# Four cross-attention layers on one core: the weighing of a batch in one piece, and one Q tile in another slot

## The reference, cut to what matters

```python
# L0 (the first) and L3 (the last), B=16, Sq=100, Sk=361, E=256, H=16, HD=16
Q = (layer_norm(x, g, b) @ wq + bq).reshape(B, Sq, H, HD)
K = (layer_norm(ctx, g, b) @ wk + bk).reshape(B, Sk, H, HD)
V = (layer_norm(ctx, g, b) @ wv + bv).reshape(B, Sk, H, HD)
scores = einsum('bqhd,bkhd->bhqk', Q, K) / sqrt(HD)
attn = softmax(scores, axis=-1)
out = einsum('bhqk,bkhd->bqhd', attn, V).reshape(B, Sq, E)
x = x + out @ wo + bo
```

## Time and profile before

| what | value |
|---|---|
| median of 3 runs | 2113.66 us (2110.45 to 2115.55) |
| profiled execution, its own time | 2111.77 us |
| its span | 2109.8 us |
| TensorE busy (matmul) | 1983.6 us, 94% |
| VectorE, ScalarE, GpSimd busy | 1414.2 (67%), 1276.3 (60%), 562.3 us (27%) |
| L0, scores of the first to the last slot | 36.57 to 339.63 us |
| L3, scores of the first to the last slot | 1807.48 to 2093.08 us |

### The profile page before, as it was taken

The page is one execution under the profiler, slowest core; times in us unless marked ns, Lnnn a source line. Parts: engine busy times, 40 slices in busy tenths (PEclk is TensorE's granted clock), DMA queues, the critical chain, the costliest instruction groups (busy, mean ns, idle before and its releaser), DMA issues. The chain is left out here.

```text
span 2109.8 us, 50608 instructions
## 1 busy us (share of the span) xinstructions
PE 1983.6 (94%) x18664; PEld 1642.0 (78%) x18664; DVE 1414.2 (67%) x2898; ACT 1276.3 (60%) x3249; POOL 562.3 (27%) x676
## 2 busy tenths in 40 slices
PE   7999996978999999999999999999999998899997
PEld 6777775977888888888777787877878876777786
DVE  4777875544545545555577887888788874677775
ACT  3777775545555555555556665666566653677775
POOL 3323320000000000000035755766666651000000
PEclk8999998999999999999999999999999998899999
DMA  5434442021000000000001000000000001344442
GB/s 165 154 125 139 145 131 101 7 73 38 16 8 9 15 9 8 15 9 8 16 1 51 10 15 11 9 10 17 9 10 10 9 1 34 108 131 131 124 124 70
DMA packets 72858, 109.63 MB, mean 52 GB/s; under 512 B 7052, under 2 KB 62508, under 8 KB 72620
## 3 DMA queue, kind: packets, MB, share of 16 engines
q1 hardware_dynamic: 72332, 105.88, 16.5%
q10 hardware_dynamic: 288, 0.51, 0.1%
HBM read 69.18 MB, written 37.19 MB: 50 GB/s over the span
## 5 line engine op out<-in xcount | busy, mean ns | idle before, releaser
L1516 ACT ACTIVATE wide_P<-PS,MX 100x361 f32<-100x361 f32 x512 | 288.3, 563 | 407.3 <-DVE MX L1634 407.3
L1634 DVE TENSOR_REDUCE MX<-PS 100x2 f32<-100x722 f32 x256 | 231.7, 905 | 148.0 <-PE PS L1386 146.5
L615 ACT ACTIVATE L_P<-PS,MX 100x361 f32<-100x361 f32 x512 | 252.7, 565 | 122.0 <-DVE MX L745 122.0
L745 DVE TENSOR_REDUCE MX<-PS 100x2 f32<-100x722 f32 x256 | 219.6, 899 | 45.2 <-PE PS L501 44.9
L1815 POOL TENSOR_TENSOR wide_AC<-wide_T,wide_COSM 128x362 f32<-128x362 f32 x128 | 130.1, 1016 | 336.3 <-ACT wide_T L1465 334.1
L513 PE MATMUL PP<-CON,L_P 100*128 100x100 f32 x1536 | 184.1, 257 | 26.4 <-DVE L_PT L752 17.5
L513 PEld LDWEIGHTS PP<-CON,L_P 100*128 100x128 f32 x1536 | 151.2, 144 | 48.4 <-ACT L_P L615 33.7
L1395 PE MATMUL PP<-CON,wide_P 100*128 100x100 f32 x1536 | 176.5, 251 | 0.0
L1395 PEld LDWEIGHTS PP<-CON,wide_P 100*128 100x128 f32 x1536 | 161.1, 142 | 9.0 <-issue 2.3
L1409 PE MATMUL PS<-wide_PT,wide_V 128*64 128x100 f32 (+1 forms) x3072 | 161.9, 254 | 0.0
L1409 PEld LDWEIGHTS PS<-wide_PT,wide_V 128*64 128x64 f32 (+1 forms) x3072 | 136.8, 137 | 31.0 <-issue 23.3
(11 more groups left out here) (242 smaller groups left out, 5355.2 us busy)
## 6 DMA issues: line engine op xcount, KB each, us to landing
strips<-L_KS SPq DMA_DIRECT2D x256, 90.5 KB
L_KA<-strips SPq DMA_DIRECT2D x64, 362.0 KB, 3.1
C<-ctx_t SPq DMA_DIRECT2D x32, 361.0 KB, 3.1
kept<-L_CTH SPq DMA_DIRECT2D x16, 361.0 KB, 4.7
kept<-L_CTL SPq DMA_DIRECT2D x16, 361.0 KB, 5.5
L_CTH<-kept SPq DMA_DIRECT2D x16, 361.0 KB, 4.2
L_CTL<-kept SPq DMA_DIRECT2D x16, 361.0 KB, 5.0
C<-in_ctx SPq DMA_DIRECT2D x8, 256.0 KB, 3.4
```

The lines of the kernel that those rows point to most:

```text
L615: nc.scalar.activation(P[:, (4 * g + j) % 8, 0:SK], PSB[0:SQ, j, 0:SK], ACT.Exp, bias=MX[:, s % 2, 4 * q + j:4 * q + j + 1], scale=1.0).th ...
L745: nc.vector.tensor_reduce(MX[:, s % 2, 4 * q + 2 * i:4 * q + 2 * i + 2], PSB[0:SQ, 2 * i:2 * i + 2, 0:SK], AX.X, ALU.max, negate=True).the ...
L1516: nc.scalar.activation(P[:, (2 * g + i) % 4, 0:SK], PS_[i][0:SQ, 0:SK], ACT.Exp, bias=MX[:, s % 2, h:h + 1], scale=1.0, accum_out=DEN[:, s ...
L1634: nc.vector.tensor_reduce(MX[:, s % 2, 2 * p:2 * p + 2], PSB[0:SQ, 0:2, 0:SK], AX.X, ALU.max, negate=True).then_inc(Z["maxed"], 1)
```

## The change

The two halves of the weighing become one job `P` in `a_` of the second slot, directly behind the scores and ahead of `turn(g - 1, 1)`. It has 48 matmuls where there were 24 on either side of the transposes. Its waits ask for the copies of the whole batch at once. One Q tile of each batch from 1 on (tile 3 of an even batch from the second on, tile 1 of the next pair in an odd batch) leaves `b_` of the first slot for `b_` of the second. On ScalarE the eviction of `P` stays behind the four exponentials, now by a condition of its own. The order of the jobs decides the PJ banks and what `begin` waits for: `P` now waits for the reading of `O` of the same batch instead of the K tile, and the moved Q tile waits for the K tile instead of `O`.

```diff
@@ jobs_at @@
                     if s + 1 < B:
                         b_.append(("K", s + 1, 1))
+                elif q == 1 and s <= B:
+                    if s == 0:
+                        a_.append(("B", 0, 0))
+                    else:
+                        a_.append(("P", s - 1, 0))
                     if even and 2 <= s < B:
                         b_.append(("Q", s, 3))
                     if not even and s + 1 < B:
                         b_.append(("Q", s + 1, 1))
-                elif q == 1 and s <= B:
-                    if s == 0:
-                        a_.append(("B", 0, 0))
-                    else:
-                        a_.append(("P1", s - 1, 0))
-                        b_.append(("P", s - 1, 0))
                     if first and even and s + 2 < B:
                         b_.append(("X", s + 2, 0))
@@ tensor @@
-                    def weigh(key, half):
+                    def weigh(key):
...
-                        pe.wait_ge(Z["unloaded_even"], NSLOT * s + 2 * half + 2)
-                        pe.wait_ge(Z["unloaded_odd"], NSLOT * s + 2 * half + 2)
-                        dst = begin(key) if half == 0 else bank(key)
-                        for q in (2 * half, 2 * half + 1):
+                        pe.wait_ge(Z["unloaded_even"], NSLOT * s + 4)
+                        pe.wait_ge(Z["unloaded_odd"], NSLOT * s + 4)
+                        dst = begin(key)
+                        for q in range(NSLOT):
...
-                        if half:
-                            last.then_inc(Z["made"], 1)
+                        last.then_inc(Z["made"], 1)
@@ scalar, the loop over the slots @@
-                            if key[0] != "M":
+                            if key[0] not in "MP":
                                 job(key)
...
-                        for key in b_:
-                            job(key)
+                        for key in a_ + b_:
+                            if key[0] == "P" or key in b_:
+                                job(key)
```

More of the change, by code:

```diff
@@ L252, in narrow_layer @@
             PARTS = (0, 2, 1)
-            order = FIRST + [k for sl in SLOTS for part in jobs_at(*sl) for k in part if k[0] != "P1"]
+            order = FIRST + [k for sl in SLOTS for part in jobs_at(*sl) for k in part]
             job_no = {k: n for n, k in enumerate(order)}
@@ L487, in job @@
                     def job(key):
-                        {"W": biases, "C": context_turn, "K": keys, "V": values, "X": query_turn, "Q": queries, "P1": lambda k: weigh(("P",) + k[1:], 0), "P": lambda k: weigh(k, 1), "N": normal_turn,
+                        {"W": biases, "C": context_turn, "K": keys, "V": values, "X": query_turn, "Q": queries, "P": weigh, "N": normal_turn,
                          "M": output_turn, "O": project, "B": output_bias}[key[0]](key)
```

## The result

| | before | changed |
|---|---|---|
| median | 2114.11 us (4 runs, 2110.45 to 2115.55) | 2134.76 us (4 runs, 2131.51 to 2136.07) |
| ratio | 1 | 1.0098, 95% interval 1.0081 to 1.0116 |
| profiled execution, span | 2109.8 us | 2129.4 us |
| TensorE busy | 1983.6 us (94%) | 1975.6 us (93%) |

The change costs 1.0%, 20.6 us by the medians and 19.6 us by the spans. TensorE is busy 8 us less and the kernel is 20 us longer: no work was added, waits were.

What follows compares the result with a forecast made beforehand. TensorE leads, relaying slots with VectorE's copy out of PP. L0 adds 11.9 us and L3 6.2 (11.5 - 5.3), 18.1 in all: profiled 2111.8 becomes 2129.9, plus 1.9 for the median, said as 2132 us; range 2119 to 2142.

Steps and rivals of the forecast that it cites:

- The Q tile leaves the first slot for nothing: First slots: TensorE is freed 0.73 us, but the turn waits for VectorE's copy; gain 1.1 us at most, taken as 0.
- The weighing of 2.17 us: Second slots: first half 1.17 us plus 48 passes at 21 ns, 1.0 us; bounds 2.0 and 2.34 us.
- Second slots held by the copy, 5.03 us, and 5.07 with X: Second slots, L0 and L3: turn-copy-turn chain 5.03 us against TensorE's list of 4.67; with X that list binds, 5.07.
- The rival in which TensorE's list binds: Second slots: 4.67 instead of 5.03 us in 24 slots, 8.6 us less, about 2121 us in all; chance 0.12.
- The third slot of odd batches in L0, 0.43 us: Q tile's low part and two statistics delay the maxima; 0.43 us on each slot held by VectorE, six times.
- the 2.6 of the sum: L0, third slots of odd batches 1 to 11: 0.43 us six times, 2.6 us in all.
- The transfers absorbed, 5.3 us: L3, fourth slots: longer batches let contexts from DRAM arrive in time, so all 5.3 us of TensorE's waits go.
- 11.9 forecast: L0 in all: second slots with X 2.6, without X 6.7, third slots 2.6 us.
- 11.5 in the sum: L3, second slots of batches 1 to 15: 0.77 us longer each; less 5.3 of absorbed waits, 6.2 us for L3.
- waits for transfers that stay: L3: SP's chain through DRAM slows along with the batches, nothing is absorbed, 5.3 us more, 2137 us; chance 0.2.
- the whole tile given back: First slots: without waiting for the copy, 28 shrink by 0.73 us each, 20.4 us, about 2111.5 us; chance 0.06.
- the compensation: Later slots have room that the first two lack, and the time comes out within the measurement; chance 0.05.

Runs made afterwards that it cites:

- the copy was moved: Changed kernel with VectorE's copy of the transposes ahead of the addition of O in first slots; ratio 1.0048 to the kernel before.
- one piece only: Kernel before with the weighing in one piece, the Q tile staying in the first slot; ratio 1.0101, median 2140.3 us beside 2116.8.
- the turn ahead: Changed kernel with the second slot ordered scores, Q tile, turn, weighing in one piece, X; ratio 1.006 to the kernel before.
- the tile only: Kernel before with the Q tile moved to the second slot, the weighing staying in two halves; ratio 1.0041, median 2127.0 us beside 2116.8.
- the early fetch: Kernel before with L3's fetch of a later context issued some 7 us earlier in SP's list, ahead of the strips' landing; ratio 0.9976.
- both edits: Kernel before with context moments and x normalizing behind the first slot's copy, and L3's context fetch earlier in SP's list; ratio 0.9945, median 2105.2 us.
- the changed kernel with the early fetch: Changed kernel with L3's context fetch issued earlier in SP's list; ratio 1.01 to the kernel before, median 2137.8 us.

## Why the prediction was right

The forecast was 2132 us with a profiled execution of 2129.9; measured were 2134.8 and 2131.5.

- *The Q tile leaves the first slot for nothing.* Right: 5.19 and 4.54 us, and 4.86 and 4.21 once the copy was moved. The step that made the prediction was to add 0.15 us to the copy's end and find the turn standing there already.
- *The weighing of 2.17 us.* Measured 2.21 (264.55 to 266.76). The floor of 25 ns that the Trainium skill states ("TensorE: Matmul & The Clock Gate", section "Wait — 56ns, not 53.3ns?") does not hold for this run of passes: 96 of them last 2.28 us, (2.28 - 0.25)/95 = 21 ns apart.
- *Second slots held by the copy, 5.03 us, and 5.07 with X.* Measured 5.06 and 5.10. The rival in which TensorE's list binds fell with one piece only (without its Q tile that list has 0.7 us less and the slot is no shorter) and with the turn ahead (4.75 us).
- *The third slot of odd batches in L0, 0.43 us.* This term of the sum was wrong: measured 0.01. The maxima do start later, 0.90 us after the scores and not 0.63. But I took VectorE's own list to hold that slot to its end, and its copy waits for TensorE's turn. Before, then changed, L0 batch 11:

```profile
264.84 0.68 PE L513 MATMUL PP<-CON,L_P 100*128 100x100 f32 x6
264.99 0.42 DVE L704 TENSOR_TENSOR L_ON<-PJ,RDEN 100x256 f32<-100x256 f32 x1
265.56 0.81 PE L394 MATMUL PJ<-CON,L_CN 128*128 128x128 f32 x6
```

```profile
271.51 0.68 PE L511 MATMUL PP<-CON,L_P 100*128 100x100 f32 x6
271.90 0.42 DVE L703 TENSOR_TENSOR L_ON<-PJ,RDEN 100x256 f32<-100x256 f32 x1
272.24 0.77 DVE L751 COPY L_PT<-PP 128x600 f32<-128x600 f32 x1
272.48 0.81 PE L393 MATMUL PJ<-CON,L_CN 128*128 128x128 f32 x6 [0.29 <-DVE L_ON L703]
```

  The turn ends at 265.52 and 272.19, and the copy starts 0.04 and 0.05 us later; before, the division had been done at 265.41. So the 0.27 us of delay go into slack. But the job `C` behind the turn waits for the division, 0.29 us, and by it the maxima of the fourth slot start 1.37 us after their scores, not 1.25: the fourth slot is 5.05 us against 4.93 (in batch 9 it is the third that has the 0.1 us). That makes some 0.6 us in all for the 2.6 of the sum. In the kernel with the tile only, the maxima are 0.75 us late and 0.49 us of it are paid: the mechanism is there, its slack is about 0.25 us.
- *The transfers absorbed, 5.3 us.* Right, shown by the early fetch, which gains in one kernel and not in the other.
- *Missed: the tails.* The wait for all copies at once costs 1.15 us where nothing else is left to do, and the lower clock adds 2.2 us in this profile. L0's tail has the same wait of 1.1 us.
- *The total is in part luck.* Its parts agree less well than the sum does. L0 came out at 10.2 us for 11.9 forecast. L3 came out at 10.2 for 6.2: 2.6 are the clock in batch 0, and of the other 7.7 the second slots have 12.6 (11.5 in the sum, and two stops of TensorE, 0.65 us, are in them), the fourth slots -5.8 (-5.3 in the sum), first and third slots 0.9. The tail adds 3.3 that the sum did not have, and the start and the middle, nothing in the forecast, are 4.1 shorter. These errors leave 1.5 us between 18.1 and 19.6. What the forecast got right by its mechanism are the distances in the steady slots.

The rivals: waits for transfers that stay fell (none in the profile), the whole tile given back fell (first slots unchanged), and so did the compensation.

## What to carry to other kernels

Where two engines hand a buffer back and forth, find the job that writes it and the job that empties it, and add the signal's way to the end of the latter; if the next start stands there, work taken from the other engine gives nothing. A long job put ahead of the hand-over delays everything that the other engine has to do behind it, while the same job behind the hand-over hides the copy. A wait that a longer kernel no longer shows was not removed, it will be back as soon as the kernel is made faster: mend both together, as the version with both edits does.

## What the runs showed of the hardware

- From the end of VectorE's copy to the start of the waiting TensorE transposes are 0.14 to 0.16 us in the steady slots of every kernel here. A copy that waits for six transposes starts 0.04 us behind their end, which is 0.72 to 0.78 us behind their start at a clock of 1.00 and 1.24 us at 0.50.
- The same work at the two clocks: six transposes last 0.68 to 0.73 us at 1.00 and 1.2 us at 0.50, the weighing in one piece 2.28 us at 1.00 and 4.23 us in the tail of the kernel with one piece only, at a mean of 0.51.
- TensorE sometimes stops, nearly always within a weighing, although it waits for nothing that is shown. It does so a few times in a run, by 0.15 to 2.2 us, at places that change between profiles; the first row is of the changed kernel. The second is the longest, in the changed kernel with the early fetch: its slot takes 8.15 us for 5.06, and the next 6.82 for 4.71 while the granted clock averages 0.61 (1847.5 to 1856.3 us), so the stop costs more than twice its length. The weighing has the shortest instructions, a weight load and a matmul every 21 ns. Whether the supply of instructions is the cause was not tried.

```profile
108.82 0.70 PE L447 MATMUL PJ<-L_PT,L_V 128*32 128x100 f32 x18 [0.80 <-issue]
1845.83 0.89 PE L447 MATMUL PJ<-L_PT,L_V 105*32 105x100 f32 x29 [2.22 <-issue]
```
